# First attention as one pipeline of query tiles, third stage with its projections between transposes and value products

## The reference, cut to what matters

```python
x = x + _layernorm(_L0_attn_ref(_layernorm(x), ...))   # first stage
x = x + _layernorm(_L0_ffn_ref(_layernorm(x), ...))    # second stage
x = x + _layernorm(_L1_attn_ref(_layernorm(x), ...))   # third stage
```

```python
qkv = jnp.einsum('bsd,ed->bse', x, W_qkv) + b_qkv
q, k, v = jnp.split(qkv, 3, axis=-1)
score = jnp.where(causal, jnp.einsum('bqd,bkd->bqk', q, k), -jnp.inf)
attn = jax.nn.softmax(score / math.sqrt(ATTN_DIM), axis=-1)
y = jnp.einsum('bqk,bkd->bqd', attn, v)
```

## Time and profile before

| | |
|---|---|
| median of 3 runs | 6315.5 us (6315.34 to 6328.09) |
| profiled execution | 6313.83 us, its span 6312.0 us |
| first stage in the trace | first matrix product at 16.93 us, last addition to `x` ends at 397.4 us |
| third stage in the trace | first statistics at 784.54 us, last addition to `x` ends at 971.1 us |
| busy over the whole span | PE 84%, PEld 61%, DVE 57%, ACT 37%, POOL 40% |

### The profile page before, as it was taken

How to read it: one execution, slowest core, us unless ns; L and a number is a source line. 1 busy time by engine, 2 the same in 40 slices (tenths; PEclk the granted TensorE clock), 3 DMA queues, 4 the chain that set the end, 5 groups by cost and what they waited for, 6 DMA issues and landing times. The chain is left out here.

```text
span 6312.0 us, 183438 instructions
## 1 busy us (share of the span) xinstructions
PE 5286.4 (84%) x72156; PEld 3821.8 (61%) x72156; DVE 3573.1 (57%) x9528; ACT 2311.8 (37%) x4102; POOL 2502.6 (40%) x2792
## 2 busy tenths in 40 slices
PE   4569767888866888988988889888679999787998
PEld 3434344555544777777777777777446666576776
DVE  4531256778775655655655565556545455675333
ACT  3432234666642333333333333333213333111333
POOL 1210013444444666666666666666410000574000
PEclk7779978999987999999999999999889999898999
DMA  0000001000000000000000000000010000000000
GB/s 18 0 19 0 2 0 41 0 0 0 0 1 14 11 11 11 11 11 11 11 13 11 11 11 11 11 11 11 9 41 0 0 0 0 4 1 28 0 0 13
DMA packets 29529, 57.57 MB, mean 9 GB/s; under 512 B 7312, under 2 KB 14240, under 8 KB 28704
## 3 DMA queue, kind: packets, MB, share of 16 engines
q1 hardware_dynamic: 28960, 48.86, 2.5%
HBM read 46.75 MB, written 2.10 MB: 8 GB/s over the span
## 5 line engine op out<-in xcount | busy, mean ns | idle before, releaser
L617 PEld LDWEIGHTS psum<-m_wd,m_h 128*128 128x128 f32 x6144 | 810.3, 193 | 484.7 <-issue 483.6
L617 PE MATMUL psum<-m_wd,m_h 128*128 128x128 f32 x6144 | 823.7, 277 | 92.3 <-remote 65.5
L2077 POOL TENSOR_TENSOR e_kd<-e_kd,e_tail 128x512 f32<-128x512 f32 x325 | 368.7, 1134 | 566.6 <-PE psum L2184 553.3
L607 PE MATMUL psum<-xT,m_wa 128*128 (+1 forms) x1032 | 549.4, 615 | 8.5 <-remote 8.5
L607 PE MATMUL psum<-xT,m_wb 128*128 (+1 forms) x1032 | 537.3, 603 | 0.0
L784 DVE SCALAR_TENSOR_TENSOR m_acc<-psum,m_combine,m_acc 128x128 f32<-128x128 f32 x1440 | 403.3, 342 | 224.9 <-PE psum L617 210.0
L544 POOL TENSOR_TENSOR m_h<-m_td,m_tb 128x512 f32<-128x512 f32 x258 | 328.6, 1274 | 480.1 <-DVE m_tb L812 480.1
L2214 PE MATMUL psum<-e_T,e_N 64*64 64x32 f32 x10400 | 403.2, 231 | 66.1 <-remote 65.2
L2214 PEld LDWEIGHTS psum<-e_T,e_N 64*64 64x64 f32 x10400 | 367.0, 147 | 112.8 <-issue 110.0
L2184 PE MATMUL psum<-e_kd,e_k 64*64 64x64 f32 x10400 | 415.4, 235 | 1.2 <-issue 0.8
L143 POOL TENSOR_SCALAR m_post_rstd<-m_post_mv 128x4 f32<-128x4 f32 x27 | 6.2, 228 | 991.0 <-DVE m_post_mv L133 991.0
(11 more groups left out here) (432 smaller groups left out, 11999.7 us busy)
## 6 DMA issues: line engine op xcount, KB each, us to landing
e_w<-in_e_w SPq DMA_DIRECT2D x66, 321.0 KB, 2.9
m_wa<-in_m_wa SPq DMA_DIRECT2D x12, 512.0 KB, 6.7
m_wd<-in_m_wd SPq DMA_DIRECT2D x12, 512.0 KB, 8.0
m_wb<-in_m_wb SPq DMA_DIRECT2D x8, 512.0 KB, 8.4
f_h<-in_f_h SPq DMA_DIRECT2D x2, 1024.0 KB
out<-x SPq DMA_DIRECT2D x1, 2048.0 KB, 8.7
f_w<-in_f_w SPq DMA_DIRECT2D x3, 256.0 KB
g_w<-in_g_w SPq DMA_DIRECT2D x3, 256.0 KB
```

The source lines that it names most:

```text
L607: pe.matmul(c.ps[i][:], w[q][:, j, :], xb, start=True, stop=True).then_inc(a_ready[i], 1)
L617: r = pe.matmul(c.ps[4 + e % 2][:, t * P:(t + 1) * P], h[:, u % DEPTH, t * P:(t + 1) * P], wd[u // UQ][:, u % UQ, :], start=(m == 0 and t ...
L2077: return g.tensor_tensor(both_odd(dst[:], m), both_odd(src[:], m), gate.unsqueeze(1).broadcast_to((P, 2, nb, m)), ALU.mult)
```

## The change

Both functions are rewritten; nothing else in the program is.

In the first stage the loops over batches are gone from all engines. Straight code runs over `N = 32` query tiles of all batches, and each engine has its own list of what it does beside tile n: scores of tile n+1, values of tile n-1, transposes of tile n, and at fixed places of the four the parts for the next batch. `xn`, `xTp`, `qT`, `kz`, `vz`, `pT` and `o` have two buffers, so that `memset` of `kz` and `vz` clears twice as much. The input is turned through bank 2 instead of bank 7, the output through bank 3 into bank 2. The value products of a tile go to bank 6 or 7 and are divided tile by tile. Semaphores count upward through the stage instead of being cleared after each wait.

In the third stage the loops are gone as well. TensorE makes the projections of batch b+1 between the transposes and the value products of batch b; the norm of an input is made two batches ahead, its statistics three ahead, and `Post` of a batch is done in the next one. The input is turned once and copied once (before: twice, to `pre_xTs` and to `xT`).

```diff
 def stage_attn0(core):
-    kz = st.sb("kz", [P, H // 2, QB + L])
-    vz = st.sb("vz", [P, NB, H // 2, PW])
+    qT, kz = st.sb("qT", [P, 2, L]), st.sb("kz", [P, 2, HP, QB + L])
+    vz = st.sb("vz", [P, 2, NB, HP, PW])
...
         @block.gpsimd
+            for n in range(N):
+                b, t = n // TB, n % TB
+                if n + 1 < N:
+                    shifted(n + 1)
+                if t == 2 and b:
+                    post.pool(g, ch)
+                if t == 2 and b + 2 < B:
+                    n1.pool_rstd(g, ch)
...
         @block.tensor
-            with pe.Fori(0, B) as b:
...
+            turn_input(0)
+            project(0)
+            turn(0)
+            scores(0)
+            turn_input(1)
+            for n in range(N):
+                b, t = n // TB, n % TB
+                if t == 1 and b:
+                    turn_output(b - 1)
+                if t == 2 and b + 1 < B:
+                    turn(b + 1)
+                if n + 1 < N:
+                    scores(n + 1)
+                if t == 0:
+                    project_v(b)
+                if n:
+                    values(n - 1)
+                if t == 0 and b + 1 < B:
+                    pe.wait_ge(vz_ready, b + 1)
+                    project(b + 1)
+                transposes(n)
+                if t == 1 and b:
+                    output(b - 1)
+                if t == 3 and b + 2 < B:
+                    turn_input(b + 2)
...
+            def turn(b):
+                pe.wait_ge(qk_ready, b + 1)
+                if b >= 2:
+                    pe.wait_ge(y_read, b - 1)
...
         @block.scalar
+            for n in range(N):
+                b, t = n // TB, n % TB
+                if t == 0:
+                    values(b)
+                if t == 1 and b:
+                    copy_output(b - 1)
+                if t == 1 and b + 1 < B:
+                    roots(b + 1)
+                if t == 2 and b + 1 < B:
+                    queries(b + 1)
+                    keys(b + 1, range(HP // 2))
+                probs_turned(n)
+                if n + 1 < N:
+                    probs(n + 1)
+                if t == 0 and b + 1 < B:
+                    squares(b + 1)
+                if t == 2 and b + 1 < B:
+                    keys(b + 1, range(HP // 2, HP))
+                if t == 3 and b + 2 < B:
+                    copy_input(b + 2)
...
         @block.vector
+            for n in range(N):
+                b, t = n // TB, n % TB
+                ch.reset()
+                if t == 1 and b + 1 < B:
+                    mean_squares(b + 1)
+                if n + 1 < N:
+                    masked(n + 1)
+                if n:
+                    weighted(n - 1)
+                if t == 0 and b + 1 < B:
+                    unscaled(b + 1)
+                if t == 1 and b + 1 < B:
+                    scaled(b + 1)
+                if t == 1 and b:
+                    result(b - 1)
+                if t == 2 and b:
+                    post.dve_stats(v, ch, lambda t: y[:, t, :])
+                if t == 2 and b + 2 < B:
+                    input_stats(b + 2)
+                if t == 3 and b + 2 < B:
+                    input_norm(b + 2)
+                if t == 3 and b:
+                    post.dve_add(v, ch, b - 1, lambda t: y[:, t, :])
 def stage_attn1(core):
...
         @block.scalar
-            with a.Fori(0, B) as b:
...
-                a.activation(q[:], c.ps[0][:], ACT.Identity, bias=bq[:])
+            for b in range(B):
+                probs(b, 3)
+                probs(b, 2)
+                a.wait_ge(pt3_ps, b + 1)
+                a.activation(prT[:, 1, :], c.ps[5][:], ACT.Copy).then_inc(pt3_ready, 1)
+                probs(b, 1)
+                probs(b, 0)
+                if b + 1 < B:
+                    queries(b + 1)
+                    keys(b + 1)
+                if b + 2 < B:
+                    copy_input(b + 2)
...
         @block.vector
+            for b in range(B):
+                ch.reset()
+                for qb in ORDER:
+                    maxima(b, qb)
+                if b:
+                    result_stats()
+                if b + 2 < B:
+                    input_norm(b + 2)
+                turned(b, 2)
+                if b + 3 < B:
+                    input_stats(b + 3)
+                turned(b, 1)
+                if b + 1 < B:
+                    values(b + 1)
+                turned(b, 0)
+                if b:
+                    post.dve_add(v, ch, b - 1, lambda t: y[:, t, :])
+                result(b)
```

More of the change, by code:

```diff
@@ L1073, in _ @@
+            values(N - 1)
+            turn_output(B - 1)
+            output(B - 1)
+            pe.wait_ge(s_free, N + 1)
+            pe.wait_ge(qk_read, B)
+            pe.wait_ge(y_read, B)
+            for sem in (xn_ready, xT_ready, qk_read, qk_ready, kz_ready, vz_ready, s_free, p_ready, pt_ready, o_ready,
+                        oT_ready, y_read):
+                pe.sem_clear(sem)
         @block.scalar
         def _(a):
[L1075 to L1082 removed]
@@ new lines, in keys, with values @@
+            def keys(b, heads):
+                a.wait_ge(k_turned, b + 1)
+                for h in heads:
+                    r = a.activation(kz[:, b % 2, h, QB:], c.ps[3], ACT.Copy, scale=hm[:, h:h + 1])
+                if h + 1 == HP:
+                    r.then_inc(kz_ready, 1)
+            def values(b):
+                a.wait_ge(v_ps, b + 1)
+                for h in range(2):
+                    r = a.activation(vz[half(h), b % 2, :, :, h * (HD + 1):h * (HD + 1) + HD],
+                                     c.psum[half(h), 2:4, :].rearrange("p a (j i d) -> p (a j) i d", i=HP, d=HD), ACT.Copy)
+                r.then_inc(vz_ready, 1)
@@ L1120, in _ @@
             st.wait_loads(a)
[L1121 to L1147 removed]
+            copy_input(0)
@@ new lines, in _ @@
+            squares(0)
+            roots(0)
+            queries(0)
+            keys(0, range(HP))
+            copy_input(1)
+            probs(0)
+            for n in range(N):
+                b, t = n // TB, n % TB
+                if t == 0:
+                    values(b)
[15 more added lines that the diff above has]
+                    copy_input(b + 2)
@@ new lines, in queries, with keys, values @@
+            def queries(b):
+                pe.wait_ge(xT_ready, b + 1)
+                pe.matmul(c.ps[3][:], wq[:], xT[:, b % 2, :], start=True, stop=True).then_inc(q_ps, 1)
+            def keys(b):
+                pe.matmul(c.ps[2][:], wk[:], xT[:, b % 2, :], start=True, stop=True).then_inc(k_ps, 1)
+            def values(b):
+                for t in range(TB):
+                    r = pe.matmul(c.ps[1][:, t * P:(t + 1) * P], xT[:, b % 2, t * P:(t + 1) * P], wv[:], start=True, stop=True)
+                r.then_inc(v_ps, 1)
@@ new lines, in _ @@
+            st.wait_loads(a)
+            copy_input(0)
+            queries(0)
+            keys(0)
+            copy_input(1)
+            for b in range(B):
+                probs(b, 3)
[4 more added lines that the diff above has]
+                probs(b, 0)
+                if b + 1 < B:
+                    queries(b + 1)
+                    keys(b + 1)
+                if b + 2 < B:
+                    copy_input(b + 2)
```

626 lines of the change are left out of this document (280 added, 346 removed).

## The result

The changed kernel takes **6251.17 us**, the median of five runs (6221.95 to 6257.77), against 6324.88 for the kernel before in the same comparison: a ratio of 0.9881, 95% interval 0.9863 to 0.9898. One execution of the kernel before took 8019.74 us; it counts in that median, which is 6320.19 without it, and not in the ratio. Forecast were 6258 us, 6234 to 6286. The time was right, but by luck: the two stages together gained 26 us more than the sum says, and an error of 19 us the other way lies outside them.

A forecast was written before the change was run, and what follows sets the result against it. Both stages were taken as bound by waits, no engine near full. Profiled 6313.8 less 60.5 (third stage) plus 3.2 (first) gave 6256.5; with the median 1.7 above the profiled execution, 6258 us, range 6234 to 6286.

The forecast's parts named there:

- the sum: Whole kernel: profiled 6313.8 less 60.5 for the third stage plus 3.2 for the first, 6256.5, then 6258 us.
- the last of the sum: Whole kernel: the median of the runs stands 1.7 us above the profiled execution, taking 6256.5 to 6258.
- the 14.2: Third stage, us a batch with VectorE as bound: 12.4 work, 1.5 standing between dependent instructions, a short wait for GpSimd's root.
- VectorE busy over 85%: Third stage, a sign to look for: VectorE busy over 85% of a batch, with first scores 14.2 us apart.
- the tail: Third stage: the last batch runs alone, taken as 19.5 us against 20.4 before, its projections being long done.
- 17 at half clock: Third stage: TensorE's work in a batch at half clock, 17 us, against 10 to 11 at full clock.
- The walk: First stage: dependent steps from one batch's first scores to the next's, together 44.2, taken as 44.0 us against 41.9.
- The first stage gains as well: First stage: norm starts ahead of the subtraction, or TensorE stays at 2.4 GHz; 41 us a batch, total 6238, chance 0.2.
- Straight code: wrong at 0: Both stages: writing out the loops put at 0 us, between 0 and a cost of 9 us for fetching.
- Half clock in both stages: Both stages: TensorE stays at half clock, batches of 17.3 us in the third and 46 in the first, 6294, chance 0.1.
- Stalls by fetching: TensorE's straight code in the first stage: 30 more blocks at 2 us cost 60; 6318 us or more, chance 0.03.
- the rival that ties VectorE to TensorE in the third stage: Third stage: copies of blocks 2 to 0 queue behind the norm, value products wait; batch of 16, 6271 us, chance 0.15.

The follow-up runs named there:

- the second: The changed kernel run again against the kernel before, nothing altered: 6257.18 us, ratio 0.9896 (0.9879 to 0.9913).
- the straight run with the old order: The kernel before with the batch loops of both stages written out on four engines, order unchanged: 6317.19 us, ratio 0.9987.
- the kernel with both edits: The changed kernel; first stage with all eight key copies first, input statistics and norm earlier, and a smaller clear of keys: 6183.70 us, ratio 0.9791.

## Why the prediction was right, and where it was not

**The total.** Sum and result differ by 7 us, but three errors cancel. The first stage was 20 us too long in the sum (+3.2 forecast, -17.1 between its ends in the traces), the third 5.4 too long (-60.5 against -65.9), and against that the rest of the program stood longer by the median than in the profile I had summed from: 6313.83 less 83 is 6231, the runs say 6251 and 6257. That the three cancel is luck. The runs show the touched stages fixed and experts and recurrence scattering by 30 us together; the trace of before that I worked from had 3404 us there, its repetition 3425. The step that failed is the last of the sum, "the median of the runs stands 1.7 above the profiled one", from three runs: over 19 runs the median stood 10 above. By the ratios the change is worth 75 us in the first comparison (64 to 87) and 66 in the second (55 to 77), against the 83 of the stages. The first interval holds the 83 and the second does not, and single executions scatter by more than the 8 to 17 us that are missing. Whether the changed program has more than its share in the untouched stages is not settled.

**Third stage: nearly the right size, but VectorE is not its bound.** Forecast: VectorE becomes the bound, batches of 14.2, first scores 11.6 us behind the first statistics, the first two batches 24, one table load, 126 us. Measured: 13.65, 12.2, 22.0, one, 120.7. The terms of the 14.2 were off both ways. The 12.4 us of work overlap now, since independent instructions follow each other: the trace has 11.50 busy, and gaps of 0.7, not 1.5. But VectorE waits 1.46 for TensorE, on which the sum had nothing, and this step failed in its mechanism: what I took for VectorE's own 14.2 is the ring over VectorE, ScalarE and TensorE. "VectorE busy over 85%" came out as 84 in the middle of the stage, and as 69% in the last batch of the same length. That 11.50 of work and 1.46 of waiting come near my 12.4 and 1.5 of gaps is luck. VectorE becomes the bound only when norm and addition leave the ring, as the run with the addition moved shows. Of the tail, 19.5 was forecast and 18.3 measured (869.38 to 887.64). One sentence was wrong: the table load was not on the chain before, it had 4 us of cover. The batch was built from what VectorE does and did not need it; the way from the first statistics to the first scores did, 12.9 less 1.3, and came out at 12.2. TensorE's "17 at half clock" does not follow from its row either: 10 to 11 at full clock are some 21 at half. No batch ran there; the traces have 9.47 us busy at 1.00 and 10.72 at 0.87.

**First stage: the ring was right, its length was not.** The walk gave 44.2 (its last item adds up to 8.56, not 8.4), the trace 41.1. Step by step, from 137.04 to 178.12:

| steps | forecast | trace |
|---|---|---|
| scores; mask and maximum | 4.9 | 4.7 |
| subtraction and held norm | 3.2 | 2.8 |
| input turned, scores, value projection | 6.4 | 5.1 |
| value copy; projection | 4.55 | 4.3 |
| bias, clip, squares | 4.3 | 3.8 |
| sum to output bias | 8.4 | 8.3 |
| turn and scores; last tile and keys | 12.5 | 12.0 |

The term mis-sized most is the value projection: 3.3 in the earlier trace rows, 2.14 now. TensorE has by then worked for 2.9 us since its idle time (144.58 to 147.52), where the projection of the earlier trace rows came 1.9 us after an idle time; that the clock rose in between is read from the length alone. The rest is spread thin, mostly over handoffs: 0.05 to 0.1 us where I took 0.15. The rival "The first stage gains as well" has the right numbers, ring 41 and 17 us less, but only half of its reason: the norm does not start ahead of the subtraction, it is held as forecast (2.09 us), and TensorE idles as forecast. Moving norm and key copies out shortened batches by 2.3 and 3.8 us, as a ring does. Also, I compared with 41.9 us where the mean of the seven intervals before is 42.5, and the first interval and the last batch took 36.8 and 36.6 us instead of 39 and 39; the last interval took 42.5. First scores at 59.08 were forecast at 58.6.

By the Trainium skill (SBUF — State Buffer, SBUF: two separate sides) the scaling of queries and keys would wait for a subtraction, 0.3 to 0.4 us by my estimate. The trace agrees in kind: 1.44 us beside the subtraction against 1.22 alone, 0.22 more.

**Straight code: wrong at 0.** It is worth 7.8 and 5.9 us; my bounds reached only to the side of a loss. About half of the first stage's 17 us is the loop, not the new order. From the straight run with the old order to the changed kernel, the order gives 69 us, 60 of them in the third stage.

**Rivals that fell.** Half clock in both stages: third at 0.87, scores 2.32 us. Stalls by fetching: three instruction packets came in a batch of the first stage, beside running engines. Of the rival that ties VectorE to TensorE in the third stage only the batch of 16 fell: the tie exists and holds the batch, through the value copy and not through the copies that I had named, and it is 13.65 long.

## What to carry to other kernels

Walk the ring of the new order step by step and look for work that stands in it only by its place in a queue: two edits of a few lines, found by that walk, gave more than the first stage's rewrite. A busy share of 84% does not make an engine the bound: compare two batches in which it has different work. Ask of a wait on the old path what else was late at that moment, as the table load shows. And before a sum is compared with a median, compare the untouched stages of two traces: here they moved by 30 us, while the rewritten stages repeated within 0.5 in the same kernel and within 2 in all kernels that had them unchanged.

## What the runs showed of the hardware

- The end of a loop's turn cost VectorE 0.34 to 0.56 us (0.58 against 0.24 ahead of the value copy, 0.70 against 0.14 ahead of the statistics), with no instruction packet beside it.
- TensorE's clock is a term of its own in short stages: with 1.2 us less idle time ahead of the transposes (1.63 instead of 2.83) five of six batches of the third stage had a granted clock of 1.00 instead of 0.87, and the same query projection took 1.02 instead of 1.91 us. Idle time alone does not decide it: the batch from 800.50 had the same 1.63 and a clock of 0.87.
- VectorE's norm is held by GpSimd's subtraction in each meeting looked at: 2.09 us for the input's, and 2.09 for the result's in the kernel with both edits, against 1.11 alone.
- Two untouched stages took 867.0 to 886.0 and 2525.5 to 2545.8 us over all traces of this study, at granted clocks of 0.93 to 0.96.
